# Layer 0's dst one-hot, hotT: scalar_tensor_tensor with a broadcast operand for tensor_scalar with two per-partition scalars

## What is computed

```
edge_in  = concat([x[src], x[dst], edge_features])        # per edge
h        = relu(edge_in @ We1 + be1)                       # 32 wide
edge_msg = relu(h @ We2 + be2)                             # 128 wide
h2       = relu(concat([x[dst], edge_msg]) @ Wn1 + bn1)    # 64 wide
node_msg = relu(h2 @ Wn2 + bn2)                            # 128 wide
agg      = segment_sum(node_msg, dst)
```

## Time and profile before

| | us |
|---|---|
| median of 3 runs | 8148.01 |
| lowest and highest run | 8145.53, 8149.95 |
| span of the profiled execution | 8149.0 |
| busy in it: PE, PE weight load | 6825.6, 5276.0 |
| busy in it: DVE, ACT, POOL | 3995.9, 1919.9, 6074.5 |
| layer 0's gathers, first to last start | 145.7 to 4082.3 |
| layer 1's gathers, first to last start | 4166.5 to 8098.9 |

### The profile page before, as it was taken

The page is one execution under the profiler, slowest core; times in us unless marked ns, Lnnn a source line. Parts: engine busy times, 40 slices in busy tenths (PEclk is TensorE's granted clock), DMA queues, the critical chain, the costliest instruction groups (busy, mean ns, idle before and its releaser), DMA issues.

```text
span 8149.0 us, 187072 instructions
## 1 busy us (share of the span) xinstructions
PE 6825.6 (84%) x52884; PEld 5276.0 (65%) x52884; DVE 3995.9 (49%) x13480; ACT 1919.9 (24%) x4919; POOL 6074.5 (75%) x6335
## 2 busy tenths in 40 slices
PE   5999999999999999999967777777778877777777
PEld 4666666666666666666646666666666666666665
DVE  7333333333333333333365555555555556555554
ACT  2333333333333333333330000000000000000001
POOL 5777777777777777777757777777777777777776
PEclk7999999999999999999979888888888888988898
DMA  6333333333333333333322222222222222222222
GB/s 141 82 83 82 81 83 82 83 82 83 82 83 82 82 83 82 83 83 82 82 61 53 53 53 53 53 53 52 53 53 53 53 52 53 52 53 53 53 53 72
DMA packets 797549, 566.94 MB, mean 70 GB/s; under 512 B 481443, under 2 KB 671019, under 8 KB 797292
## 3 DMA queue, kind: packets, MB, share of 16 engines
q0 software_dynamic: 200192, 256.65, 14.6%
q1 hardware_dynamic: 597340, 310.10, 14.5%
HBM read 544.45 MB, written 21.68 MB: 69 GB/s over the span
## 4 chain that ended last, share of the span: by engine, by line
PE 32%; issue 24%; POOL 21%; DMA 20%; DVE 1%; POOLq 1%; SPq 0%; ACT 0%; DVEq 0%; ACTq 0%
PE bank L1130 19%; POOL shared L549 17%; DMA shared<-p_tab,idx 11%; DMA rows_place<-h_tab,idx 6%; PE bank L1143 5%; POOL rows_place L549 4%; PE bank L1132 3%; DMA idx<-in_src_t 2%; PE bank L1054 2%; PE bank L1145 1%; PE bank L1061 1%; PE bank L1080 0%; DMA x_in<-in_x 0%; PE bank L1071 0%; DVE stats L744 0%
## 5 line engine op out<-in xcount | busy, mean ns | idle before, releaser
L549 POOL DMA_INDIRECT shared<-p_tab,idx x3128 | 2984.1, 954 | 959.8 <-issue 826.7
L549 POOL DMA_INDIRECT rows_place<-h_tab,idx x3128 | 2978.3, 952 | 964.3 <-issue 804.4
L1130 PE MATMUL bank<-shared,rows_place 128*128 128x256 f32 x6256 | 1842.2, 446 | 860.4 <-issue 748.1
L1130 PEld LDWEIGHTS bank<-shared,rows_place 128*128 128x128 f32 x6256 | 1296.4, 218 | 1126.6 <-issue 782.8
L959 DVE TENSOR_SCALAR shared<-iota_key,key,w_f 128x256 f32<-128x256 f32 x3128 | 1139.1, 425 | 745.3 <-PE bank L1132 633.1
L704 ACT ACTIVATE x_in<-bank 128x256 f32<-128x256 f32 x782 | 300.8, 385 | 3591.9 <-PE bank L1132 3264.7
L1061 PE MATMUL bank<-h_sb,w_tile 128*128 128x128 f32 x6256 | 907.7, 288 | 22.3 <-DVE h_sb L870 0.8
L1061 PEld LDWEIGHTS bank<-h_sb,w_tile 128*128 128x128 f32 x6256 | 758.5, 191 | 232.4 <-DVE h_sb L870 232.1
L1080 PE MATMUL bank<-wn_half,h_sb 128*128 128x128 f32 x6256 | 890.3, 285 | 0.0
L870 DVE TENSOR_SCALAR h_sb<-bank 128x128 f32<-128x128 f32 x782 | 228.2, 292 | 1315.8 <-PE bank L1054 1294.3
L1143 PE MATMUL bank<-x_in,w_rel_sb 128*128 128x64 f32 x6256 | 862.8, 296 | 0.0
(11 more groups left out here) (105 smaller groups left out, 5379.0 us busy)
## 6 DMA issues: line engine op xcount, KB each, us to landing
rows_place<-in_dst_c SPq DMA_DIRECT2D x782, 192.0 KB
shared<-in_edge_cols SPq DMA_DIRECT2D x782, 128.0 KB
shared<-p_tab,idx POOLq DMA_INDIRECT x3128
rows_place<-h_tab,idx POOLq DMA_INDIRECT x3128
idx<-in_src_t SPq DMA_DIRECT2D x1564, 2.0 KB
qr_w<-qr_tab SPq DMA_DIRECT2D x782, 18.0 KB
x_in<-in_x SPq DMA_DIRECT2D x14, 448.0 KB, 4.7
h_tab<-x_in SPq DMA_DIRECT2D x14, 448.0 KB, 3.0
```

The costliest lines, as they stand in the source:

```text
L549: pool.indirect_dma_start(out=rows_of[s][:, t, :], out_offset=None, in_=table, in_offset=bass.IndirectOffsetOnAxis(ap=idx[s][:, t:t + 1], ...
L1130: pe.matmul(bank[s][:, 0:RW], rows[s][:, t, :], hot_rel[s % 2][:, t, :], start=(t == 0), stop=(t == TC - 1))
```

## The change

In build_hot, the one instruction that makes hotT is another instruction. The value, the output, the order on DVE and every wait stay. The first input and the first scalar stay. The second scalar, row_f[:, 0:1] (one value for each partition), becomes the second tensor input: the same value read 512 times through an access pattern with a step of 0.

```
-                dve.tensor_scalar(hotT[s % 2][:, :], dst_wide[s], base_c[0:3 * W, ds(c.i, 1)], row_f[:, 0:1],
-                                  ALU.subtract, ALU.is_equal).then_inc(hot_built[s], 1)
+                dve.scalar_tensor_tensor(out=hotT[s % 2][:, :], in0=dst_wide[s], scalar=base_c[0:3 * W, ds(c.i, 1)],
+                                         in1=row_f[:, 0:1].broadcast_to([3 * W, CH]), op0=ALU.subtract, op1=ALU.is_equal)\
+                   .then_inc(hot_built[s], 1)
```

## The result

| | before | changed |
|---|---|---|
| median, us | 8146.77 (8142.51 to 8150.25, 6 runs) | 8250.97 (8221.28 to 8288.15, 6 runs) |
| ratio | | 1.013, 95% interval 1.0112 to 1.0149 |
| profiled execution: span | 8149.0 | 8236.8 |
| layer 0's gathers, first to last start | 3936.6 | 4027.5 |
| layer 1's gathers, first to last start | 3932.4 | 3929.0 |

The loss is 104 us in the median and 88 between the two profiled executions. All of the latter lies in layer 0: its gathers stretch over 90.9 us more, layer 1's over 3.4 less. The changed kernel's runs also spread over 67 us, those of before over 8.

A forecast was written before the change was run, and what follows sets the result against it. POOL's back-to-back gathers were taken to bound layer 0, the only layer touched. Terms 58.0 - 10.2 - 5.3 gave +42.5 us, a replay +50; +47 was taken on 8148, giving 8195, range 8145 to 8255.

The forecast's parts named there:

- a wider window: hotT against layer 0's gathers: window widened by 0.2 us of fixed time to 0.73, near +140 us.
- POOL paces layer 0: Layer 0: POOL runs gathers back to back, 1.259 us each, so every delay of a gather is paid in full.
- The instruction's own time: hotT on DVE: the new instruction takes 0.75 us, 0.21 us longer than the old.
- its cover on DVE: DVE after hotT: the 0.21 us lies under L876's 0.68 us wait for PE and costs nothing; uncovered, at most 164 us.
- The price of an offset: Layer 0's gathers: hotT starting at offset -0.61 to -0.08 from a gather adds offset + 0.61 us.
- second window: Old hotT starting 0.29 to 0.42 us into a gather delays it; the change removes this, 5.3 us.
- The two SBUF inputs as its cause: hotT and L839: two tensor inputs hold off POOL's short access near a gather's start for as long as they stream.
- Terms 2 and 3: Layer 0's gathers: the old hotT's two windows go, saving 10.2 us (88 starts) and 5.3 us (71 starts).
- Term 1: Layer 0's gathers: first window grows to 0.53 us; 301 of 782 old hotT starts lie there, costing 58.0 us.
- The replay of +50: Layer 0's 782 chunks replayed with each one's own delay from last gather to hotT: 68 us after, 18 now, +50.
- self-locking: Layer 0: a delayed chunk's next hotT comes later, starts creep up the window; +180, 8255 to 8328, chance 0.08.
- The weighed rule: hotT against gathers: colliding DVE and GpSimd instructions exclude each other for their whole length; +350, 8498, chance 0.02.

The follow-up runs named there:

- the row number in PSUM: Changed kernel with the second input of hotT's scalar_tensor_tensor (row number, step 0) read from PSUM, so one SBUF input: 8125.44 us, ratio 0.9976 to the kernel before.
- the two runs from PSUM: Changed kernel with hotT's second input read from PSUM, 8125.44 us; the same with the ramp of hot (L839) also from PSUM, 8111.46 us.

## Why the prediction fell short

The time lies in the range of 8145 to 8255, and the sign is right, but the loss is 104 us where 47 was forecast. That the median is still in the range is luck: the range went up to 8255 for a wider window, which did not come. By the prediction's steps:

- POOL paces layer 0, and a delayed gather is paid in full: held. 91 us more in the gathers' durations, 90.9 in their span.
- The instruction's own time, 0.75, and its cover on DVE: held, at 0.741 and no cost, shown by the row number in PSUM, which has both and loses nothing.
- The price of an offset: held, window -0.61 to -0.08, one for one, second window gone. The two SBUF inputs as its cause: shown by the two runs from PSUM.
- Terms 2 and 3, the old windows, 15.5 us: the right size. The run with the row number in PSUM gained 20.3; the median gather is 3 ns shorter in it as well, which no term had.
- Term 1, the 301 chunks in the window and 58.0 us: this is the step that failed. It took the starts of before as given. They were 450, and 114.8 us; with that the prediction's own sum gives 114.8 - 15.5 = +99, and layer 0 grew by 91. The replay of +50 failed in the same way: it kept each chunk's delay from last gather to hotT as measured and let only the fourth gather's own delay move it, later. In fact the third gather's delay moves it, the other way: a gather held off by 0.41 us cuts the follow time by about 0.33 (3.00 against 3.32 to 3.36), because relu_h1 comes only 0.11 us later for a fourth gather that starts 0.42 later. That puts the next hotT again ahead of the next third gather. 274 chunks of this kind carry 91.7 us.
- The rival "self-locking" had the right idea with the wrong sign of movement, and a chance of 0.08; its 8255 to 8328 begins 4 us above the median, and three of the six runs lie in it.
- The weighed rule, SBUF — State Buffer, section "SBUF: two separate sides", of the Trainium skill: who collides is as it says, in that one input moved to PSUM ends the collisions. For how long is not: a hold of a gather ends after 0.53 us of hotT's 0.74, and POOL's own part in it, by what L839 waited, under 0.07 us of a gather's 0.95.

## What to carry to other kernels

Before a DVE instruction gets a second SBUF input, look at whether GpSimd issues indirect DMAs beside it and paces the loop; price it by the length of one hold, by its place against the gathers, and not by its duration. A price curve read from offsets is good, but the offsets of the kernel before are not those of the kernel after when the delay feeds back on them: ask which way a delay moves the next collision. In this kernel a small operand that is read over and over did better in a free bank of PSUM: with three of them there it took 8097 us, and the kernel before 8155 beside it.

## What the runs showed of the hardware

- A scalar_tensor_tensor of 96x512 with both inputs in SBUF or with the second in PSUM takes 741 and 737 ns, and only the former holds a gather off, by up to 0.54 us.
- A tensor_scalar of 128x256 with its input moved from SBUF to PSUM goes from 425 to 536 ns, 0.11 more.
- A pause on POOL that made a chunk's period 0.19 us longer went with a follow time 0.65 us shorter in the mean (3.84 to 3.19), in one pair of traces. What varies in the follow time is the time from the fourth gather's start to the landing of its rows.
- The same program, the kernel before, had medians of 8146 to 8155 us in some sets of runs and of 11653 to 11917 in others, at a granted clock of 0.93 and of about 0.75; with one chip number both times were seen.
